# Two transposes per sample taken from TensorE: 32 by 32 blocks moved by transfers and turned by VectorE

## The reference, cut to what matters

```
x1 = layernorm(x + L0(x))     # L0: concat(x, x*s, x*s*s, ...) @ W + b, s: row sums of the graph
x2 = layernorm(x1 + o2)       # o2 = L1(x1): A_hat @ x1, @ W1, batchnorm, relu, @ W2, batchnorm
h  = relu(adj @ (x2 @ Wg0 + bg0)); h = relu(adj @ (h @ Wg1 + bg1))
for p in 1, 2, 3, 4:          # 10 cells in time
    h[last node of each window of p nodes] = LSTM_p(the window)
x3 = layernorm(x2 + h)
out = layernorm(x3 + y)       # y = L3(x3), 8 Euler steps:
#   y = x3 @ fc_w.T + fc_b; 8 times: y += dt * (alpha * 0.5 * (adj @ y - y) + y @ w_eff - y + x3)
```

## Time and profile before

| | us |
|---|---|
| median of 3 runs | 919.82 (918.21 to 920.14) |
| the profiled execution | 921.33 |
| its span, first to last instruction | 919.5 |
| TensorE busy in the span | 885.8 (96%) |
| VectorE busy | 664.0 (72%) |
| ScalarE busy | 564.0 (61%) |
| GpSimd busy | 339.1 (37%) |

### The profile page before, as it was taken

One profiled execution on the slowest core, in us unless ns is written; L12 is line 12 of the kernel. 1 busy time (PEld: TensorE's weight loads), 2 busy tenths in 40 slices (PEclk: granted clock), 3 DMA queues, 4 the chain that ended last, 5 costly groups with the idle time before them and its releaser, 6 DMA issues.

```text
span 919.5 us, 14510 instructions
## 1 busy us (share of the span) xinstructions
PE 885.8 (96%) x4966; PEld 768.8 (84%) x4966; DVE 664.0 (72%) x1583; ACT 564.0 (61%) x1233; POOL 339.1 (37%) x550
## 2 busy tenths in 40 slices
PE   8999999988989999999999999999999999999996
PEld 6888985466877799888989998898989899978986
DVE  5988886886687766667677667767676777665744
ACT  5676766935755674677377547745763775466341
POOL 3777875621023520342153136214421631340221
PEclk9999999999999899999999999999999999999999
DMA  5412201320110101012001201010120001001000
GB/s 188 148 60 71 74 29 69 138 70 1 35 59 1 35 12 47 1 47 65 5 13 35 70 1 36 24 58 1 47 69 1 12 12 47 1 11 36 1 24 23
DMA packets 26594, 38.54 MB, mean 42 GB/s; under 512 B 3333, under 2 KB 12422, under 8 KB 26010
## 3 DMA queue, kind: packets, MB, share of 16 engines
q1 hardware_dynamic: 26088, 36.05, 11.7%
q10 hardware_dynamic: 434, 1.57, 0.5%
HBM read 21.89 MB, written 15.73 MB: 41 GB/s over the span
## 4 chain that ended last, share of the span: by engine, by line
PE 47%; DVE 12%; ACT 8%; POOL 7%; issue 5%; ACTq 0%; DVEq 0%; POOLq 0%
PE psum L141 14%; PE psum L143 13%; PE psum L142 13%; PE psum L1892 2%; PE psum L1893 2%; ACT gate L1465 2%; PE psum L1896 2%; POOL out_rstd L1398 1%; DVE x_stats L1644 1%; DVE x L1666 1%; DVE in_h L1634 1%; POOL node_l L1416 1%; POOL x_rstd L1398 1%; ACT raw L1496 1%; ACT gate L1468 1%
## 5 line engine op out<-in xcount | busy, mean ns | idle before, releaser
L1465 ACT ACTIVATE gate<-psum,gate_bias 128x256 f32<-128x256 f32 (+2 forms) x296 | 143.4, 556 | 62.0 <-PE psum L1896 53.0
L141 PE MATMUL psum<-in_h,wih_h 128*128 128x256 f32 (+2 forms) x312 | 106.8, 342 | 7.3 <-DVE in_l L1638 5.0
L143 PE MATMUL psum<-in_h,wih_l 128*128 128x256 f32 (+2 forms) x312 | 103.5, 332 | 0.0
L142 PE MATMUL psum<-in_l,wih_h 128*128 128x256 f32 (+2 forms) x312 | 102.8, 329 | 0.0
L1432 POOL TENSOR_TENSOR gate<-in_h,in_l 128x512 f32<-128x512 f32 x14 | 17.9, 1307 | 157.5 <-DVE in_l L1638 157.5
L141 PEld LDWEIGHTS psum<-in_h,wih_h 128*128 128x128 f32 x312 | 58.8, 188 | 19.2 <-DVE in_l L1638 9.1
L1468 ACT ACTIVATE gate<-cell 128x512 f32<-128x512 f32 (+2 forms) x80 | 40.3, 503 | 51.2 <-DVE cell L1622 39.7
L1619 DVE TENSOR_TENSOR gate<-gate 128x256 f32<-128x256 f32 (+2 forms) x48 | 24.0, 501 | 61.3 <-ACT gate L1465 61.2
L142 PEld LDWEIGHTS psum<-in_l,wih_h 128*128 128x128 f32 x312 | 59.0, 189 | 5.5 <-issue 0.5
L143 PEld LDWEIGHTS psum<-in_h,wih_l 128*128 128x128 f32 x312 | 58.8, 189 | 4.6
L141 PE MATMUL psum<-e_h,shared 128*128 128x384 f32 x180 | 61.4, 341 | 0.2
(11 more groups left out here) (403 smaller groups left out, 2887.2 us busy)
## 6 DMA issues: line engine op xcount, KB each, us to landing
x_spill<-x SPq DMA_DIRECT2D x30, 256.0 KB, 2.0
xt<-in_x_t_dram SPq DMA_DIRECT2D x16, 256.0 KB, 2.6
raw<-x_spill SPq DMA_DIRECT2D x16, 256.0 KB, 2.9
o_spill<-xt SPq DMA_DIRECT2D x14, 256.0 KB, 2.0
xt<-o_spill SPq DMA_DIRECT2D x14, 256.0 KB, 3.3
x<-x_spill SPq DMA_DIRECT2D x14, 256.0 KB, 3.5
out_dram<-raw SPq DMA_DIRECT2D x14, 256.0 KB, 2.3
raw<-in_adj_t_dram ACTq DMA_DIRECT2D x1, 1024.0 KB, 9.2
```

What stands on the lines that cost most here:

```text
L141: pe.matmul(dst, lh, rh, start=start, stop=False, **kw)
L142: pe.matmul(dst, lh, rl, start=False, stop=False, **kw)
L143: return pe.matmul(dst, ll, rh, start=False, stop=stop, **kw)
L1465: nc.scalar.activation(gate[q][:, 0:n], banks[GATE_BANK[q]][:, 0:n], ACT.Tanh if q == 2 else ACT.Sigmoid, bias=gate_bias[:, p - 1, q:q + 1 ...
```

## The change

The 128x128 turn is split in two: transfers bring each 32 by 32 block to the place of its mirror image, and one VectorE instruction turns all blocks in place. It is used for o2 of samples 6 to 15 (`by_blocks`) and for x3 of groups 1 to 6 (`moved`). Where neither holds, TensorE turns as before.

For o2 the load itself moves the blocks: four transfers of 32 partitions in place of one of 128, each with pieces of 128 bytes. Since a partition then holds one of four features, the normalization is four instructions with columns that are prepared once (`norm2_blocks`, by four small matmuls). For x3, SP issues 16 transfers from x3 to a new buffer `turning` once x3 is normalized (`x3move`), and VectorE turns it (`x3turn`) before ScalarE and VectorE split it (`x3high`, behind `power2` now).

The lists change with it: `turn_0` stands behind cell 0 instead of cell 1, `prep_1` of ScalarE behind cell 2 instead of cell 4. Of the lists, two lines:

```diff
-        FILL_DVE = [[], ["ysum_1", "ysum_0", "turn_0"], ["x3t_0", "x3sum_1", "outsum"], ["power1_0", "power2_0", "gather0_0"],
+        FILL_DVE = [["turn_0"], ["ysum_1", "ysum_0"], ["x3t_0", "x3sum_1", "outsum", "x3turn_0"], ["power1_0", "power2_0", "x3high_0", "gather0_0"],
-        FILL_SP = [["prep_1"], [], ["norm_0"], ["out_0"], ["ahead_0"], [], ["norm_1"], ["out_1"], ["x3load"], [], []]
+        FILL_SP = [["prep_1"], [], ["x3move_0", "norm_0"], ["out_0"], ["ahead_0"], ["x3move_1"], ["norm_1"], ["out_1"], ["x3load"], [], []]
```

The core of the rest:

```diff
+        def moved(g):
+            return not isinstance(g, int) or 1 <= g < G - 1
+        def by_blocks(n):
+            return not isinstance(n, int) or n >= 3 * GB
@@ SP, prep @@
+                if by_blocks(n):
+                    by_node = o2_dram[b].rearrange("(a i) (t q k) -> q i t a k", a=blocks, q=blocks, k=side)
+                    for q in range(blocks):
+                        rows = o2[j][side * q:side * (q + 1), :].rearrange("i (t a k) -> i t a k", a=blocks, k=side)
+                        sp.dma_start(rows, by_node[q]).then_inc(front_loaded[j], 16)
+                else:
+                    sp.dma_start(o2[j], o2_dram[b]).then_inc(front_loaded[j], 16)
@@ SP @@
+            def x3move(g, j):
+                if not moved(g):
+                    return
+                n = GB * g + j
+                sp.wait_ge(x3_ready, n + 1)
+                sp.wait_ge(power_lo[1 - j], BABY * (g + j))
+                for a in range(quarters):
+                    for b in range(quarters):
+                        rows = turning[quarter * a:quarter * (a + 1), :].rearrange("k (t b i) -> k t b i", b=quarters, i=quarter)[:, :, b, :]
+                        sp.dma_start(rows, x3[quarter * b:quarter * (b + 1), j, :, quarter * a:quarter * (a + 1)]).then_inc(x3_moved, 16)
 @@ ScalarE, prep @@
+                if by_blocks(n):
+                    act.wait_ge(columns_kept, 1)
+                    for a in range(blocks):
+                        part = o2[j].rearrange("p (t a k) -> p a t k", a=blocks, k=side)[:, a, :, :]
+                        ins = nc.scalar.activation(part, part, ACT.Identity, scale=norm2_blocks[:, a, 0:1], bias=norm2_blocks[:, a, 1:2])
@@ VectorE, turn and x3turn @@
+                if by_blocks(n):
+                    dve.wait_ge(normed2, n)
+                    chain.link(nc.vector.transpose(o2[j], o2[j]))
+                    nc.vector.tensor_tensor(flat(x2[j]), o2[j], flat(x2[j]), ALU.add).then_inc(x2_summed, 1)
+            def x3turn(g, j):
+                if moved(g):
+                    n = GB * g + j
+                    dve.wait_ge(x3_moved, 16 * quarters * quarters * (n - GB + 1))
+                    nc.vector.transpose(turning[:], turning[:]).then_inc(x3_turned, 1)
```

More of the change, by code:

```diff
@@ L865, in _ @@
             pe.wait_ge(c_w, 48)
-            pe.matmul(tile(banks[3][:], 0), ones[0:1, :], bias0[:], start=True, stop=True).then_inc(bias_spread, 1)
+            pe.matmul(tile(banks[3][:], 0), ones[0:1, :], bias0[:], start=True, stop=True).then_inc(pe_setup, 1)
             pe.wait_ge(weights_ready, 1)
@@ L1213, in outputs @@
             return [(source[:, 0:n].rearrange("p (j w) -> p j w", j=GB), mod4(twos)[:, 3, :, :])]
-        FILL_PE = [[], ["giant_2", "giant_3", "giant_0", "giant_1", "turn_0"], ["x3t_0", "power1a_0"],
-                   ["power1b_0", "power2_0", "gather0_0"], ["coefs0_0", "weight0_0"], ["coefs1_0", "turn_1"],
+        FILL_PE = [[], ["giant_2", "giant_3", "giant_0", "giant_1"], ["x3t_0", "power1a_0"],
+                   ["power1b_0", "power2_0", "gather0_0"], ["coefs0_0", "weight0_0"], ["coefs1_0"],
@@ L1226, in second_half @@
                     ["gather0_1", "input_0"], ["weight0_1", "coefs0_1"],
                     ["coefs1_1", "gather1_1", "innersum_0", "weight1_1", "x3add", "input_1", "innerlow_0", "innersum_1", "x3first", "innerlow_1"]]
-        FILL_POOL = [[], ["x3split_0", "turn_0"], ["norm_0", "outsum", "x3sum_1"], [], [], ["x3split_1", "turn_1"], ["norm_1"], [], [], [],
+        FILL_POOL = [["turn_0"], ["x3split_0"], ["norm_0", "outsum", "x3sum_1"], [], [], ["x3split_1", "turn_1"], ["norm_1"], [], [], [],
@@ L1372, in x3load @@
                     sp.dma_start(flat(x3[:, j, :, :]), x2_dram[GB * g + j]).then_inc(x3_loaded, 16)
-            run(None, {"prep": prep, "ahead": prep, "norm": norm, "out": out_piece, "outhalf": out_half, "x3load": x3load},
+            run(None, {"prep": prep, "ahead": prep, "norm": norm, "out": out_piece, "outhalf": out_half, "x3load": x3load, "x3move": x3move},
                 START_SP, ONCE_SP, FILL_SP, FILL_SP, FILL_SP, TAIL_SP)
@@ L2043, in weff, with block_columns @@
                 pe.matmul(tile(banks[0][:], 0), lws[:], lw[:], start=True, stop=True).then_inc(weff_done, 1)
+            def block_columns():
+                pe.wait_ge(lws_ready, 2)
+                for a in range(blocks):
+                    mm = pe.matmul(banks[0][:, P + 2 * a:P + 2 * (a + 1)], bp[:, 5 + a, :], norm2[:], start=True, stop=True)
+                mm.then_inc(weff_done, 1)
             def product(k, t):
```

127 lines of the change are left out of this document (83 added, 44 removed).

## The result

The changed kernel takes 936.32 us, median of 4 runs (934.54 to 938.15), beside 919.98 (918.21 to 920.80) for the kernel before on the same chip. The ratio is 1.0182, 95% interval 1.0165 to 1.0199: slower by 16.3 us. The forecast was 930.0 with a range of 917 to 944, so slower was right, and the time is inside the range, with 6 us of the size missing.

What follows compares the result with a forecast made beforehand. TensorE, busy 83.30 of 83.70 us a step, was taken as the bound. Five steps of +2.25 us (+11.2) and -0.9 in the last gave +10.3: 919.82 to 930.1 us, own range 926 to 938, wider range 917 to 944.

Steps and rivals of the forecast that it cites:

- one of its own signs of being wrong: VectorE's cell 3: the forecast would be wrong if the landing of the moves is what it waits for.
- turn_0 ahead of cell 1: VectorE before cell 1: 2.23 us inserted against 0.45 us spare, so TensorE's cell 2 starts 1.4 us later.
- x3's low half: Behind cell 2: TensorE waits for GpSimd's x3split_0 0.2 to 0.8 us, 0.6 taken; bounds nothing and 1.
- turn_1 at cell 7: VectorE between cells 5 and 6: no spare time, so 0.7 us more wait at TensorE's cell 7, near 1.6 altogether.
- the forecast of a step: Middle step: +1.4 at cell 2, -0.44 for x3t_0, +0.6 low half, +0.7 at cell 7, +2.25 us; range 1.95 to 2.65.
- The price of four transposes: TensorE: each group of four transposes removed frees 0.44 us; 22 groups give at most 9.7 us.
- The cover just holds: cost nothing, with a knee at an issue time of about 0.5 us: x3turn_0 before cell 3: sixteen issues at 0.475 us land in time; above the knee each 0.1 us costs 1.5 a step.
- Rival 1: Moves land late, VectorE stands before cell 3: 2 to 3 us more in six steps, 942 to 948; chance 0.15.
- The last loop step has no turn ... two groups, -0.9: Last loop step: TensorE's 2.11 us wait at cell 4 is for a chain that starts earlier, saving 0.9 us.
- prep_1 in ScalarE's cell 2: Four-part normalization, 1.64 us, held hidden where ScalarE's wait for x2's shift goes; under 1 us each if uncovered.

Runs made afterwards that it cites:

- run 4: Changed kernel with x3 copied by four transfers of 32 partitions in place of 16, blocks not moved (wrong x3): 930.3 us.
- run 5: Changed kernel with x3 through DRAM, one store and four loads that place the blocks, 5 issues in place of 16: 928.9 us.
- run 8: Changed kernel with the second o2 tile of each group loaded whole and turned by TensorE: 934.8 us.
- run 2: Kernel before with only x3 moved, by sixteen transfers, and turned by VectorE; o2 turned by TensorE: 924.8 us.
- run 9: Kernel before with only x3's first tile of each group moved through DRAM and turned by VectorE: 920.2 us, ratio 0.9988.
- run 3: Changed kernel with turn_0 back behind ysum in cell 1, sixteen transfers kept: 935.3 us.
- run 11: Changed kernel with turn_0 back behind ysum in cell 1 and x3 through DRAM: 929.7 us.
- run 6: Kernel before with only x3 (both tiles) moved, through DRAM, and turned by VectorE: 919.5 us, ratio 0.9992.
- run 10: Kernel before with only o2's first tile of each group by blocks, turn_0 behind ysum: 922.6 us.
- run 1: Changed kernel with x3 turned by TensorE again, only o2 by blocks, turn_0 ahead of cell 1: 928.2 us.
- run 7: Changed kernel with only the first tiles of o2 and x3 changed, x3 through DRAM, turn_0 behind ysum: 923.6 us.
- run 12: As run 4, but x3's first tile is copied by two transfers of 64 partitions, its second by one of 128: 930.2 us.

## Why the prediction was right, and where it was not

The direction and most of the size are right, for the mechanism that it gave: work inserted on VectorE ahead of two hand-overs. Runs 4 and 5, without the late moves, have 930.3 and 928.9 us, near the forecast of 930.0, and two misses cancel in part there: in run 4 the five steps cost 9.6 us in place of 11.2, and the last step saves 0.1 in place of 0.9. The measured 936.3 holds something that the forecast put at nothing, and one of its own signs of being wrong is there: the landing of the moves is what VectorE's cell 3 waits for. That 936.3 is still inside 926 to 938 is luck, since the upper end stood for a transpose of 1.4 us, which takes 0.70.

- **turn_0 ahead of cell 1.** Right in place and size: 2.26 us put in (2.23), 1.60 to 1.64 us of wait at cell 2 (1.8), and cell 2 1.44 us later than before (1.4). The VectorE transpose was taken from the tensor_tensor row and is 0.70 us. The estimate of 1.24 us from the Trainium skill (VectorE: DVE Perf Modes, "The three transpose paths") does not hold for this float32 tile.
- **x3's low half.** A wait of 0.6 us forecast, 0.33 in the trace.
- **turn_1 at cell 7.** A wait of 1.13 us for 1.6 forecast, and the steps of run 8 show that it hangs on turn_1.
- **Without the moves' lateness** the forecast of a step was 2.25 us more. Runs 4 and 5 show 1.9 to 2.0. The difference is at cell 7: TensorE is 1.61 us late at cell 4 in run 5 (1.56 forecast), but VectorE's cell 5 only 1.28, because ScalarE had waited 0.65 us ahead of an output in cell 3 before and waits there no more. So cell 7 comes 1.9 us later and not 2.25. The range of 1.95 to 2.65 for a step also left out its own bound of nothing for x3's low half, which gives 1.65. The price of four transposes was right: TensorE's next work comes 0.40 to 0.44 us earlier without them (runs 2 and 9), though its busy time falls by 0.31 only (1.25 for sixteen).
- **The step that failed: "The cover just holds: cost nothing, with a knee at an issue time of about 0.5 us".** An issue every 0.64 us came in place of one every 0.475. The seven small loads of the earlier trace rows were the wrong row; the same trace has two issues of 0.60 and 0.64 us, of 128 KB loads, at 2.89 and 3.54 us. The late moves cost 6.0 us by run 4 and 7.4 by run 5. Rival 1 had named this ("at 0.6 us each ... 2 to 3 us a step ... 942 to 948") and had 0.15. Its mechanism is what happened, and its size was too large, as the knee lies higher than 0.5: cell 4 comes 0.5 us late behind 10.25 us of issues and 1.45 late behind 11.22, so not at all up to some 9.8 us, 0.61 an issue. The last transfer landed 1.8 to 1.9 us behind its issue in steps 2 to 6, where the forecast had 2.0 to 3.5, and VectorE waits 1.8 us for cell 3's gates in any case (1.78 us in the earlier trace rows, 1.79 in run 5). A middle step paid 0.5 us, and 1.5 where one issue took 1.6 us, in place of 2 to 3.
- **"The last loop step has no turn ... two groups, -0.9".** It cost +2.8. The chain of the transfers starts 2.2 us earlier there, but it is as long, and ahead of it TensorE already waited. Of the 2.8, the longer wait is 3.83 - 2.11 = 1.7, and the rest the slower clock behind it. Without late moves (run 4) it is 73.0 us, so the saving of 0.9 did not come either: cell 4 starts 0.43 us earlier, but ScalarE now has x3high_0 ahead of that cell's gates, which start at 31.29 us behind the mark for 31.19 before, and the second group came back as wait at cell 7, 2.28 us for 1.84.
- **What I didn't see:** prep_1 in ScalarE's cell 2. The prediction held it hidden, since ScalarE waits for x2's shift there. With turn_0 early it is; with turn_0 back it is not (runs 3 and 11). That the change loses 9 us even with its transfers in time fits what the rows show of spare time: between cell 1 and cell 4, and between cells 5 and 7, the other engines' chain had at most half a us of it. Each of a step's four VectorE transposes puts 0.7 us into it and takes 0.3 to 0.4 from TensorE.

No version here beats the kernel before: runs 6 and 9 are level with it. Three things stay untried: the whole change by DRAM with turn_0 behind ysum and prep_1 in cell 4, which could take up to 1.5 us a step from run 11, to some 922 us (an estimate from its rows); o2's first tile by blocks with prep_1 in cell 4; and x3's first through DRAM with x3high_0 ahead of power1_0. By the rows above each of the last two has 0.4 us a step to win over the kernel before at most, some 2 us in all.

## What to carry to other kernels

Work that leaves an engine which is 99% busy gives its time back only where no other chain is due at the next hand-over. Read the spare time at each hand-over first, and take the length of the inserted work and not that of the removed work as the price. Where many small transfers are issued by one queue, take the time of an issue from a row of the same shape, or bound it at half as much again, and look first for a form with fewer issues: five transfers with a detour through DRAM beat sixteen direct ones by 7 to 8 us. When two edits meet in one chain, run each alone: here 7.3 and 3.9 us made 16.3.

## What the runs showed of the hardware

- A VectorE transpose in 32 by 32 blocks of 128x512 float32 in SBUF takes 0.69 to 0.71 us, as much as a tensor_tensor on the tile.
- SyncE's issue took 0.33 us for a store of 128 partitions to DRAM, and 0.59 straight behind sixteen others. Inside SBUF it took 0.51 for 128 partitions, 0.50 and 0.59 for two of 64, 0.55 and then 0.58 for four of 32 with pieces of 2 KB, and 0.60 for 32 with pieces of 128 bytes. Single ones took 1 to 1.9 us; what makes them is not shown.
- Pieces of 128 bytes inside SBUF are no load for the DMA engines: from 643 to 655 us of the changed kernel 2248 packets took 13.7% of the sixteen engines, 12 ns each.
- The granted clock can halve behind a wait of 2.1 to 2.4 us of TensorE, and need not. Behind the wait of 2.08 to 2.11 us at cell 4 in step 7 it fell in four executions (runs 5, 6, 10 and 11) and stayed in six (before, 1, 4, 7, 9 and 12); behind one of 2.34 to 2.38 us (runs 3 and 11) it fell in eight of ten steps. Windows of run 5 and run 9 in step 7, both behind a wait of 2.10 us at cell 4:

```profile
828.00:830.00 2.00, 1.65 (x6) 1.65 (x7) 2.00 (x4) 2.00 (x6) 1.76 (x4) 0.55 0.00 0
830.00:832.00 2.00, 2.00 (x9) 2.00 (x8) 0.59 (x2) 1.59 (x4) 0.14 (x1) 0.60 0.44 131
```

```profile
819.00:821.00 2.00, 1.17 (x7) 1.17 (x8) 2.00 (x5) 2.00 (x7) 1.76 (x4) 1.00 0.00 0
821.00:823.00 2.00, 1.90 (x12) 1.62 (x11) 1.06 (x2) 1.85 (x5) 0.53 (x2) 1.00 0.31 93
```

It costs the 1.1 us between 74.1 and 73.0 in the table's last column. No wait of 1.64 us or less in the steps had it behind it.
